# One-hot rows of the nodes in a graph attention layer: from VectorE's comparison to ScalarE's Abs and Relu

## What is computed

```python
for r in range(R):                      # 5 edge types, weights W_Q[r], W_K[r], W_V[r]
    mask = edge_types == r
    q, k, v = x[dst] @ W_Q[r], x[src] @ W_K[r], x[src] @ W_V[r]    # 8 heads of 16
    logits = (q * k).sum(-1) / scale + attn_bias[r]
    exp_l = where(mask, exp(logits - segment_max(logits, dst)), 0)
    attn = exp_l / (segment_sum(exp_l, dst)[dst] + 1e-12)
    out = out + segment_sum(attn * v, dst, n)
out = out @ out_proj_w.T + out_proj_b
y = layernorm(out + x) * ln_gamma + ln_beta
return layernorm(x + y)
```

## Time and profile before

| | us |
|---|---|
| median of 3 runs (lowest, highest) | 1299.65 (1297.06, 1303.98) |
| the profiled execution, device time | 1311.24 |
| its span, first to last instruction | 1309.5 |
| TensorE matmuls busy | 913.0 (70%) |
| TensorE weight loads busy | 804.1 (61%) |
| VectorE busy | 1005.1 (77%) |
| ScalarE busy | 539.0 (41%) |
| GpSimd busy | 766.5 (59%) |

### The profile page before, as it was taken

How to read it: one execution, slowest core, us unless ns; L and a number is a source line. 1 busy time by engine, 2 the same in 40 slices (tenths; PEclk the granted TensorE clock), 3 DMA queues, 4 the chain that set the end, 5 groups by cost and what they waited for, 6 DMA issues and landing times.

```text
span 1309.5 us, 18831 instructions
## 1 busy us (share of the span) xinstructions
PE 913.0 (70%) x5180; PEld 804.1 (61%) x5180; DVE 1005.1 (77%) x1855; ACT 539.0 (41%) x979; POOL 766.5 (59%) x856
## 2 busy tenths in 40 slices
PE   9933576777677767768675767566777777666677
PEld 4522565676566657667565766565666666666676
DVE  3555687777778778779777779777788798778996
ACT  5623444444444344434443444344344334343422
POOL 0076666666666656666666666656666666666630
PEclk9955555555555656555555565566555555555555
DMA  9975555555655455545554565555554445545410
GB/s 333 364 227 170 162 167 165 151 162 150 169 160 157 134 163 167 163 129 164 162 164 128 155 166 159 143 155 159 169 162 140 145 140 156 143 147 150 139 44 12
DMA packets 121375, 209.25 MB, mean 160 GB/s; under 512 B 22845, under 2 KB 79546, under 8 KB 121166
## 3 DMA queue, kind: packets, MB, share of 16 engines
q0 software_dynamic: 37632, 102.81, 27.6%
q1 hardware_dynamic: 82626, 102.94, 25.9%
q10 hardware_dynamic: 1008, 2.25, 0.5%
HBM read 176.92 MB, written 30.99 MB: 159 GB/s over the span
## 4 chain that ended last, share of the span: by engine, by line
issue 29%; DVE 29%; PE 18%; another core or an unknown queue 13%; DMA 4%; ACT 4%; DVEq 2%; POOL 1%; SPq 0%; ACTq 0%; POOLq 0%
PE pp L1813 5%; PE pp L1761 4%; DVE LW L1278 4%; DVE pool L1340 3%; DVE pool L1369 3%; DVE av L647 3%; PE pp L555 3%; DVE Tt L1256 3%; DMA rkb<-Ktab 2%; PE pp L1798 2%; DVE pool L1244 2%; DVE pool L1266 2%; DVE Mt L1355 1%; DVE Yt L1326 1%
## 5 line engine op out<-in xcount | busy, mean ns | idle before, releaser
L1653 POOL DMA_INDIRECT ring<-KVtab,kvi x784 | 754.4, 962 | 490.5 <-issue 206.2
L1761 PE MATMUL pp<-qwin,pool 128*128 128x128 bf16 x2352 | 281.7, 301 | 167.3 <-issue 126.1
L1761 PEld LDWEIGHTS pp<-qwin,pool 128*128 128x128 bf16 x2352 | 249.5, 146 | 211.0 <-issue 191.2
L1813 PE MATMUL pp<-ohn,av 128*128 128x32 f32 x1464 | 318.3, 383 | 28.1 <-issue 26.7
L1813 PEld LDWEIGHTS pp<-ohn,av 128*128 128x128 f32 x1464 | 314.1, 318 | 29.0 <-issue 26.8
L1266 DVE TENSOR_TENSOR pool<-pp,ring 128x512 f32<-128x512 f32 x196 | 133.7, 682 | 89.4 <-remote 58.8
L867 ACT ACTIVATE pool<-rkb,npid 128x512 bf16<-128x512 bf16 x196 | 139.6, 712 | 107.7 <-DMA rkb<-Ktab 70.9
L1798 PEld LDWEIGHTS pp<-sel,pool 120*128 120x128 f32 (+1 forms) x536 | 130.1, 325 | 54.3 <-issue 53.6
L1798 PE MATMUL pp<-sel,pool 120*128 120x24 f32 (+1 forms) x536 | 130.0, 392 | 39.7 <-issue 31.1
L647 DVE TENSOR_TENSOR av<-ring,pp 128x512 f32<-128x512 f32 x183 | 124.5, 680 | 35.2 <-remote 35.2
L871 ACT ACTIVATE pool<-pool,one 128x512 bf16<-128x512 bf16 x196 | 141.4, 722 | 6.4
(11 more groups left out here) (130 smaller groups left out, 877.1 us busy)
## 6 DMA issues: line engine op xcount, KB each, us to landing
rkb<-Ktab SPq DMA_DIRECT2D x196, 128.0 KB
mk<-Mtab SPq DMA_DIRECT2D x201, 100.2 KB
qwin<-Qfast SPq DMA_DIRECT2D x196, 96.0 KB
KVtab<-pool SPq DMA_DIRECT2D x25, 640.0 KB, 5.6
ring<-KVtab,kvi POOLq DMA_INDIRECT x784
Qfast<-pool SPq DMA_DIRECT2D x21, 480.0 KB
Qfast<-ring SPq DMA_DIRECT2D x4, 480.0 KB
xs<-in_x_b SPq DMA_DIRECT2D x5, 320.0 KB, 7.0
```

Of the source, the lines that this page charges most:

```text
L1653: e.indirect_dma_start(kv[:, home(m), j, :], None, KV, bass.IndirectOffsetOnAxis(kvi[:, 4 * q + j:4 * q + j + 1], 0)).then_inc(kv_in[m % 6 ...
L1761: last = e.matmul(pp[2 + m % 2][:, j * C:(j + 1) * C], ohr[:, m % OR, j * C:(j + 1) * C], qwin[:, m % 2, k * C:(k + 1) * C], start=(k == 0 ...
L1813: last = e.matmul(sums_at(f), weighed_at(f)[:, j, :], hot_at(f)[:, j, :], start=(j == 0), stop=(j == 3))
```

## The change

`reln` is kept in fp32, since it becomes ScalarE's per-partition bias, one column for each of the four columns of a front. `one_hot(f)` moves from VectorE's program to ScalarE's. It is now five instructions instead of one: four Abs of 128x32, |reln - io32|, each raising the new semaphore `node_dist`, then one Relu of 128x128 over all four, relu(1 - |.|), in place, raising `nodes`. The wait for `collected` goes with it. In the loop ScalarE makes the front of step s+1 as the last work of step s. Behind the loop fronts 183 to 194 are spread over ScalarE's program; `EARLY_HOT` goes from 192 to 195, so VectorE's setup makes three rows (195 to 197) instead of six, and fronts 192 to 194 are made by ScalarE too.

```diff
-IN_RING, EARLY_HOT = 183, 192
+IN_RING, EARLY_HOT = 183, 195
-        reln = sb("reln", [128, 4 * G * STREAM], BF16)
+        reln = sb("reln", [128, 4 * G * STREAM])
+            def one_hot(f):
+
+                q = quad_of(FRONT[f])
+                if f >= AR:
+                    e.wait_ge(collected, f - AR + 1)
+                for j in range(4):
+                    e.activation(hot_at(f)[:, j, :], io32[:, :], ACT.Abs, bias=reln[:, 4 * q + j:4 * q + j + 1],
+                                 scale=-1.0).then_inc(node_dist, 1)
+                e.wait_ge(node_dist, 4 * (f + 1))
+                e.activation(hot_at(f), hot_at(f), ACT.Relu, bias=one[:, 0:1], scale=-1.0).then_inc(nodes, 1)
+
...
                 for g, k in plan.root.get(s, []):
                     root(g, k)
+                if s + 1 < END:
+                    for f in plan.fronts.get(s + 1, []):
+                        one_hot(f)
...
             keys(NQ - 1)
+            one_hot(183)
             exp_shift(63)
             keep_turned(63)
+            one_hot(184)
             log_total(63)
             exp_weigh(63)
+            one_hot(185)
             exp_shift(64)
             keep_turned(64)
             keep_weights(62)
+            one_hot(186)
+            one_hot(187)
             log_total(64)
             exp_weigh(64)
             keep_weights(63)
+            one_hot(188)
             exp_shift(65)
+            one_hot(189)
+            one_hot(190)
             log_total(65)
             exp_weigh(65)
+            for f in range(191, EARLY_HOT):
+                one_hot(f)
...
-            def one_hot(f):
-                if f >= AR:
-                    e.wait_ge(collected, f - AR + 1)
-                mark_nodes(e, f).then_inc(nodes, 1)
-
...
-                for f in plan.fronts.get(s, []):
-                    one_hot(f)
                 if s in plan.shift:
                     shift(plan.shift[s])
                 logits(s)
```

More of the change, by code:

```diff
@@ L522, in build @@
             sem("run_sum"), sem("full_sum"), sem("logged"), sem("normed"), sem("weight"))
-        attn, nodes, weighed, collected, added = (
-            sem("attn"), sem("nodes"), sem("weighed"), sem("collected"), sem("added"))
+        attn, nodes, node_dist, weighed, collected, added = (
+            sem("attn"), sem("nodes"), sem("node_dist"), sem("weighed"), sem("collected"), sem("added"))
         late_x, weights_kept, pool_weighed = sem("late_x"), sem("weights_kept"), sem("pool_weighed")
@@ L1477, in vector_fast @@
             sums(63)
-            one_hot(183)
             total(63)
@@ L1486, in vector_fast @@
             times_key(195)
-            one_hot(184)
-            one_hot(185)
             logits(195)
@@ L1497, in vector_fast @@
             add(182)
-            one_hot(186)
-            one_hot(187)
             norm_sum(64)
@@ L1504, in vector_fast @@
             backward(65)
-            one_hot(188)
             shift(65)
-            one_hot(189)
             add(184)
-            one_hot(190)
             add(185)
             sums(65)
-            one_hot(191)
             total(65)
```

## The result

| | us |
|---|---|
| before, median of 4 runs (lowest, highest) | 1300.74 (1297.06, 1303.98) |
| after, median of 4 runs (lowest, highest) | 1316.99 (1312.15, 1319.89) |
| ratio after to before, 95% interval | 1.0129 (1.0097 to 1.0161) |
| after, the profiled execution (its span) | 1318.51 (1316.8) |

The kernel became slower by 1.3%, 16 to 17 us. The time lies inside the predicted range (1276 to 1327) but above the forecast's own range (1293 to 1310), on the side of rival B. The forecast had called no measurable change (within 0.5%).

A forecast was written before the change was run, and what follows sets the result against it. The prediction took VectorE to pace most loop steps and TensorE's signals the rest. Relief of 14 us, ScalarE's queue at 14 and the end at 3 gave +3 us, 1303 us, called same; own range 1293 to 1310, 8-in-10 range 1276 to 1327.

The forecast's parts named there:

- rival B: ScalarE's queue: the copy-out of Q becomes the bound, 22 waits grow in full; +24 us, about 1324 us; chance 0.34.
- Part 1: VectorE's loop: 183 comparisons leave, gaining 20 us by start times, not 50 by recorded durations; counted as 14 us off.
- the list of signs: Closing list of what would show each step, such as VectorE's busy sum falling by some 54 us.
- 14 us off: VectorE's relief in the loop: 20 us of earlier starts times a pacing share of about 0.7 to 0.8.
- 14 us on: ScalarE's queue in the loop: 1.3 us per front delays copy-outs TensorE waits for; half of 29 us.
- its last sentence: Forecast is wrong if VectorE's gaps before L1266 and L1221 move with VectorE, or late keys push the queries.
- later keys have room: TensorE's queries waited for the keys' Relu only twice, 16.6 us, so delayed keys were given no cost.
- The cover before Ln and the shift's Exp: ScalarE idles 1.6 and 3.3 us before these, so they should not move; VectorE's waits stay under 25 us.
- 3 us on: Behind the loop: front 191 behind the last Exp delays the last weights' way back 4 us, less 1 gained.
- A: VectorE paces everywhere, its relief counts in full and ScalarE's additions hide; about 1278 us; chance 0.26.
- C: The diff doesn't work as told: a table load, or fp32 input makes VectorE's remaining comparisons dear; chance 0.02.

The follow-up runs named there:

- e3: The kernel before with 179 of the loop's 183 comparisons left out and nothing in their place; 1122.20 us against 1124.08, ratio 0.9986.
- e4: The kernel before with VectorE's comparisons kept and ScalarE also making the loop's five instructions into an unread tile; 1140.15 us against 1124.08, ratio 1.0139.
- e5: The kernel before, unchanged, timed beside itself for its profile under the experiments' condition; 1124.60 us against 1124.66, ratio 0.9995.
- e1: The change in the loop alone, VectorE still comparing fronts 183 to 194 behind it, against the kernel before; 1133.24 us against 1124.08, ratio 1.0083.
- e6: The whole changed kernel against the kernel before, under the experiments' condition; 1137.07 us against 1124.66, ratio 1.0111.
- e9: As e1, but the five instructions stand behind take_q, ahead of the shift's Exp or Ln; 1125.55 us against 1125.34 for the kernel before, ratio 1.0003.
- e2: The change behind the loop alone, VectorE still comparing fronts 0 to 182, against the kernel before; 1128.28 us against 1124.08, ratio 1.0035.
- e12: The changed kernel with three gathers a quad instead of four from quad 30 on; 1125.63 us against 1125.34 for the kernel before, ratio 1.0008.
- e10: As e2, but front 191 is made ahead of the last Ln; 1124.29 us against 1125.34 for the kernel before, ratio 0.9999.

## Why the prediction was partly right

**The unit costs held.** The timeline of after shows one front on ScalarE, and VectorE's three places of the earlier trace rows without the comparison. The line by itself below is of before and belongs to the last of the three.

```profile
601.27 0.94 ACT L934 ACTIVATE ohn<-io,reln 128x32 f32<-128x32 bf16 x4
...
602.25 0.40 ACT L937 ACTIVATE ohn<-ohn,one 128x128 f32<-128x128 f32 x1
...
602.55 0.71 ACT L867 ACTIVATE pool<-rkb,npid 128x512 bf16<-128x512 bf16 x1
...
609.09 0.69 DVE L1291 TENSOR_TENSOR pool<-pp,ring 128x512 f32<-128x512 f32 x1
...
609.81 0.69 DVE L1303 TENSOR_REDUCE LW<-pool 128x32 f32<-128x512 f32 x1
...
616.96 0.35 DVE L1375 TENSOR_TENSOR_SCAN Mt<-LT,Mt,pool 120x64 f32<-120x64 bf16 x1
617.34 0.28 DVE L1269 SCALAR_TENSOR_TENSOR pool<-Mt,clamp,carry 120x64 f32<-120x64 f32 x1
...
622.35 0.35 DVE L1281 TENSOR_TENSOR_SCAN Tt<-LT,Tt,pool 120x64 f32<-120x64 bf16 x1
622.62 0.66 DVE L1303 TENSOR_REDUCE LW<-pool 128x32 f32<-128x512 f32 x1
```

```profile
622.29 0.35 DVE L1256 TENSOR_TENSOR_SCAN Tt<-LT,Tt,pool 120x64 f32<-120x64 bf16 x1
```

From the first Abs to the start of the next instruction 1.28 us pass (predicted 1.3). The reduction follows the product's start by 0.72 us instead of 0.81: 0.09 gained (predicted 0.08). The shift follows the short backward piece by 0.38 instead of 0.44: 0.06 (predicted 0.05). The reduction follows the short total piece by 0.27 us where 0.45 us lay between them before (622.29 to 622.74): 0.18 (predicted 0.19). ScalarE's busy sum rose by 237.6 us (predicted about 250). VectorE's fell by 25.6, not by 54: busy time is a union of records, and where the comparison's record overlapped its neighbours' it can't fall by the comparison's whole duration. Part 1 had this right and the list of signs had not. VectorE's idle sum grew by 33 us ("30 us or more" was the sign).

By the Trainium skill, ScalarE: Activation LUTs, section "What ACT_TABLE_LOAD costs", an Abs of 32 columns with a pointer bias would be 307 ns; the group shows 307.

**The relief was mis-sized (step "14 us off"; measured 1.6 in e3, about 6 beside ScalarE's load).** The 20 us in VectorE's own time were right: it is busy 22 us less in e3. Wrong was the factor after them, the busy share of 0.7 to 0.8 as the share of steps in which VectorE paces. A busy share says how full an engine is, not how much of the time the end waits for it. The list of bounds had left out GpSimd, whose 188.8 of 300 us looked like room. Where the kernel takes 1300 us its stream does have gaps (167.1 us "remote" and 44.1 us for queries), so the 1.6 us and their cause are shown for the experiments' condition alone. What holds the relief back in the other stays open; the change as a whole costs as much in both.

**The cost of ScalarE's queue had the right size (step "14 us on"; measured 15.6 in e4).** The size was luck in part: half of the upper end of 29 us was taken with no row for the half. And it named one way, the copy-out. TensorE's waits for it in after grew by 12 us, as told (85 to 97, predicted about 100), but the waits for late queries grew as much: VectorE's from 22.2 to 34.8 us, GpSimd's from 44.1 to 55.7. The prediction had no term for late queries; its last sentence had named them as what would make it wrong. By which way they become late isn't settled. In after TensorE's queries wait longer for the keys (16.6 us in 2 cases, 27.4 in 7), which speaks against "later keys have room". Where the kernel takes 1124 us these waits hardly grow (3.7 us in e5, 6.3 in e1, 5.2 in e6), and the queries are late all the same, behind TensorE's longer waits for the copy-out (57.3, 70.0 and 69.6 us).

**The cover before Ln and the shift's Exp held.** VectorE's waits for the two in after are these, 26.5 us together where "under 25" was predicted:

```profile
DVE Yt L1346 <- ACT Tt L906: 19.7, 13, 2.5
...
DVE pool L1389 <- ACT Et L889: 6.8, 4, 2.5
```

They were longer yet in e9 (33.5 us), which lost nothing by them.

**The end held (step "3 us on"; measured 3.9 in e2).** The timeline of after has each link.

```profile
1285.88 0.79 ACT L914 ACTIVATE pool<-Yt 120x704 f32<-120x704 f32 x1 [0.96 <-DVE Yt L1346]
1286.57 0.94 ACT L934 ACTIVATE ohn<-io,reln 128x32 f32<-128x32 bf16 x4
1287.54 0.40 ACT L937 ACTIVATE ohn<-ohn,one 128x128 f32<-128x128 f32 x1
...
1288.09 1.89 PE L1822 MATMUL pp<-ohn,ring 128*128 128x32 f32 x8 [3.44 <-ACT ohn L937]
...
1290.19 0.82 DVE L1246 TENSOR_TENSOR aggT<-aggT,pp 128x32 f32 x3 [4.35 <-PE pp L1822]
...
1292.08 4.18 PE L1807 MATMUL pp<-sel,pool 120*128 120x24 f32 x24
```

TensorE waits 3.44 us for front 191. From the end of the last Exp (1286.67) to the way back 5.4 us pass, against 1.0 before (1283.81 to 1284.79): 4.4 more. From the same Exp to the end of the run it is 30.1 us against 25.7, again 4.4 more (predicted 3 to 4).

**The rivals.** A is refuted (e3, e12). B's time (1324) was 7 us too high and its side was right: it had the relief at 8 us and the copy-out at 29. What was true in it was that waits behind ScalarE's queue weigh more than the relief; its reason, the copy-out alone, was too narrow. C didn't come: ScalarE has two table loads of 1.28 us each in the whole of after, as it has in before, and VectorE's busy sum fell.

So the sum failed by one term, the relief, as far as the experiments' condition shows. With e3's 1.6 us in place of 14 it would have been 15 us on, 1315 us; with the 6 us between e4 and e1, 11 us on, 1311 us. Measured were 12.5 and 16 to 17 us on in the two conditions. That the range held says little for the mechanism: it was laid over most of both rivals. The forecast's own range is also a little narrow for its terms, a third to two thirds of 29 us, 10 to 20 us of relief and 3 us, which give 1292 to 1312.

## What to carry to other kernels

The cost of work moved from the fullest engine to an emptier one can hang on its place in the receiver's queue. Here the place decided between a loss and none: put it ahead of an instruction that waits for another engine anyway, and behind those that another engine waits for (e1 against e9, e2 against e10). Before counting a relief, look for a second stream that is back to back at its own pitch, issue gaps included, since its busy share needn't show it. And multiply a saving by no busy share: leave the work out once and time it.

## What the runs showed of the hardware

**A steady indirect gather of 128 rows costs GpSimd 1.25 us:** 0.96 us recorded and 0.30 us of issue before the next, in 703 gathers of e5.

**The same kernel took 1300 us in one set of comparisons and 1124 us in the others.** Busy times differ by far less than the time does (VectorE 1005.1 and 1000.5 us, GpSimd 766.5 and 768.9, TensorE 913.0 and 879.0), the mean granted clock is 0.560 and 0.579, and the span differs by 185 us. What differs in the traces is when signals arrive: in the first VectorE waited 171 us for "remote" signals (four rows: 58.8, 49.6, 35.2, 27.7), GpSimd 167.1 and ScalarE's copy-out 142.9 us; in the second no engine has such a row. All of these lines wait for a semaphore that TensorE raises, which fits the prediction's reading of "remote". What delays these signals wasn't tried and stays open; two chips gave the 1124 us, and which one gave the 1300 isn't known, so a difference between chips isn't ruled out. It also leaves open how the loop's loss splits in the slower condition, of which only the total (1.0129) and the end (4.4 us) are shown.
